# Cross attention and a decoded FFN on one core: another order for decoding, beginning and end

## What is computed

```
n = layernorm(x)
q = rmsnorm(n, ln_weight) @ w_q.T        # per head
k = ctx @ w_k.T;  v = ctx @ w_v.T
score = softmax(where(mask, q k^T + position_bias[h], -inf))
hid = x + n + (score @ v) @ w_out.T
W = NF4_CODE[w_codes] * absmax           # 512 x 512, blocks of 64
y = layernorm(hid)
out = hid + y @ W.T + 2 * (y @ W_a) @ W_b
```

## Time and profile before

| | us |
|---|---|
| median of 3 executions (860.21 to 862.35) | 860.31 |
| the profiled execution | 860.71 |
| its span in the trace | 858.9 |
| PE busy, matmuls | 832.1 (97%) |
| PE weight loads, beside them | 723.7 (84%) |
| DVE busy | 449.2 (52%) |
| ACT busy | 442.1 (51%) |
| POOL busy | 537.7 (63%) |
| PE: four LoRA matmul tiles from 3.58 and four from 7.16 | 3.78 and 3.62 |
| DVE idle ahead of the value splits at 18.42 | 4.52 |
| DVE idle ahead of `q_lo` at 786.09 (head 29), and of `row_scale`'s reciprocal at 792.40 (head 30) | 1.69 and 1.11 |
| ACT idle ahead of `qT` at 784.94 (head 29) | 3.17 |
| granted clock of PE, 42 to 46 and 77 to 81 us | 0.62 and 0.57 |

### The profile page before, as it was taken

One profiled execution on the slowest core, in us unless ns is written; L12 is line 12 of the kernel. 1 busy time (PEld: TensorE's weight loads), 2 busy tenths in 40 slices (PEclk: granted clock), 3 DMA queues, 4 the chain that ended last, 5 costly groups with the idle time before them and its releaser, 6 DMA issues.

```text
span 858.9 us, 15761 instructions
## 1 busy us (share of the span) xinstructions
PE 832.1 (97%) x4694; PEld 723.7 (84%) x4694; DVE 449.2 (52%) x761; ACT 442.1 (51%) x1296; POOL 537.7 (63%) x557
## 2 busy tenths in 40 slices
PE   8798999999999999999999999999999999999898
PEld 5687888988889888898889888898888888898776
DVE  4854656246543566246561565336562465534783
ACT  5655554354634656264543657356553646346632
POOL 0484758856686658857587557856588565865230
PEclk9999999999999999999999999999999999999999
DMA  8212323023321223113231132112220232211102
GB/s 329 73 41 89 96 70 98 19 72 102 91 65 52 89 64 95 31 61 95 68 96 56 53 106 89 37 52 92 69 95 23 69 95 75 92 40 50 44 13 86
DMA packets 51125, 64.98 MB, mean 76 GB/s; under 512 B 11008, under 2 KB 37248, under 8 KB 50080
## 3 DMA queue, kind: packets, MB, share of 16 engines
q1 hardware_dynamic: 51104, 64.73, 24.1%
HBM read 44.24 MB, written 4.19 MB: 56 GB/s over the span
## 4 chain that ended last, share of the span: by engine, by line
PE 49%; POOL 24%; ACT 11%; issue 5%; DVE 5%; SPq 3%; DMA 2%; POOLq 1%; ACTq 0%; DVEq 0%
PE w_ps L1157 23%; PE o_ps L1157 19%; POOL picked L528 8%; POOL level L531 6%; ACT p_blocks L649 4%; PE s_ps L1193 4%; POOL ring_lo L464 3%; PE s_ps L1199 3%; ACT p_blocks L600 2%; POOL wv_raw L454 2%; SPq L336 2%; POOL p L492 2%; DMA wv_raw<-wv_dram 1%; ACT kT L600 1%; POOL wo_lo L464 1%
## 5 line engine op out<-in xcount | busy, mean ns | idle before, releaser
L492 POOL TENSOR_TENSOR p<-pos_raw,mask_add 128x1024 f32<-128x1024 f32 x32 | 69.6, 2175 | 137.8 <-ACT p_blocks L649 137.3
L649 ACT ACTIVATE p_blocks<-p,neg_max 128x128 f32<-128x128 f32 x248 | 96.1, 389 | 84.0 <-DVE neg_max L966 78.6
L528 POOL TENSOR_SCALAR picked<-codes 128x256 f32<-128x256 int32 x112 | 124.4, 1111 | 19.4 <-POOL level L531 15.9
L531 POOL TENSOR_TENSOR level<-level,picked 128x256 f32<-128x256 f32 x112 | 89.6, 800 | 20.6 <-POOL picked L528 20.6
L464 POOL TENSOR_TENSOR ring_lo<-k_raw,ring_hi 128x256 fp32r<-128x256 f32 x105 | 77.0, 745 | 28.1 <-ACT ring_hi L600 25.1
L988 DVE TENSOR_TENSOR resid<-o_ps,resid 128x512 f32<-128x512 f32 x102 | 68.6, 686 | 43.2 <-PE o_ps L1157 43.2
L1157 PE MATMUL w_ps<-ctx_hi,ring_hi 128*128 128x512 f32 x210 | 84.7, 403 | 0.1
L1157 PE MATMUL w_ps<-ctx_hi,ring_lo 128*128 128x512 f32 x210 | 82.0, 391 | 0.0
L1157 PE MATMUL w_ps<-ctx_lo,ring_hi 128*128 128x512 f32 x210 | 81.7, 389 | 0.0
L600 ACT ACTIVATE p_blocks<-p_blocks,row_scale 128x128 f32<-128x128 f32 x248 | 77.1, 391 | 0.0
L600 ACT ACTIVATE ring_hi<-k_raw 128x256 fp32r<-128x256 f32 x105 | 38.8, 413 | 74.4 <-POOL k_raw L454 74.4
(11 more groups left out here) (222 smaller groups left out, 2310.8 us busy)
## 6 DMA issues: line engine op xcount, KB each, us to landing
pT<-p_blocks SPq DMA_DIRECT2D x496, 32.0 KB, 1.8
k_raw<-k_dram SPq DMA_DIRECT2D x16, 512.0 KB, 3.4
wv_raw<-wv_dram SPq DMA_DIRECT2D x8, 1024.0 KB, 4.8
q_raw<-q_dram SPq DMA_DIRECT2D x32, 256.0 KB, 3.2
wo_raw<-wo_dram SPq DMA_DIRECT2D x32, 256.0 KB, 4.0
resid<-x_dram SPq DMA_DIRECT2D x2, 1024.0 KB, 12.9
pos_raw<-pos_dram SPq DMA_DIRECT2D x32, 64.0 KB, 3.9
out_dram<-resid SPq DMA_DIRECT2D x8, 256.0 KB, 2.0
```

The costliest lines, as they stand in the source:

```text
L492: pool.tensor_tensor(p[:, :, :], pos, mask_add[:, :, :], ALU.add).then_inc(bias_done, 1)
L528: then(pool.tensor_scalar((level if code == 0 else picked)[:, :], codes[:, :], float(code), NF4[code], match, ALU.mult))
L531: then(pool.tensor_tensor(level[:, :], level[:, :], picked[:, :], ALU.add))
L649: e = act.activation(out(b), p[:, b, :].rearrange("p (k c) -> p k c", c=Q), ACT.Exp, bias=neg_max[:, b:b + 1], accum_out=prob_sum[:, b:b + 1])
```

## The change

Decoding: `PARTS` becomes 4, 4, 4 and 3 codes instead of 4, 6, 4 and 1, so two pick-and-add pairs move from j = 4 to the parts done at j = 1 and 2 (part 3 has three pairs where it had one, part 2 has other codes but as many).

```
-PARTS = ((0, 1, 2, 3), (4, 5, 6, 8, 9, 10), (11, 12, 13, 14), (15,))
-PART_STEP = (0, 7, 19, 27)
+PARTS = ((0, 1, 2, 3), (4, 5, 6, 8), (9, 10, 11, 12), (13, 14, 15))
+PART_STEP = (0, 7, 15, 23)
```

Beginning, the core of the diff by engine. PE (`EARLY_LORA` is 3, and with `parts=2` a key product waits for its second context split, `ctx_lo_done` 2 or 4, between its halves):

```
-            for c in range(C):
+            for c in range(EARLY_LORA):
                 lora_tile(c)
             pe.wait_ge(k_lo_done, PRODUCTS)
-            pe.wait_ge(ctx_lo_done, 2)
-            first_keys(1, 0)
+            pe.wait_ge(ctx_lo_done, 1)
+            first_keys(1, 0, parts=2)
             first_keys(0, 0)
...
+            for c in range(EARLY_LORA, C):
+                lora_tile(c)
             pe.wait_ge(wv_lo_done, PRODUCTS)
...
             turn_x(0)
-            first_values(3)
+            for b in (3, 4):
+                first_values(b)
             turn_x(1)
-            first_values(4)
+            first_values(5)
...
             scores(0, 1)
-            for b in range(5, B):
+            for b in (6, 7):
                 first_values(b)
```

```
             dve.wait_ge(x_loaded[0], 16)
             for b in range(HB):
                 tile_stats(b, 2 * b)
-            ask_layer_power(0)
+            ask_both(0)
+            for half_at in range(2):
+                split_first_values(half_at)
+            stage_factors(0)
...
+            residual_factors()
+            xn_low(0)
+
+            dve.wait_ge(x_turned, C)
+            context_sum(2, ctx_sum[0], ctx_raw[BLOCK_A])
             dve.wait_ge(ctx_sums, 3)
+            context_sum(4, ctx_raw[BLOCK_B], ctx_sum[1])
+            split_first(4, ctx_lo[:, 1, :, :], ctx_sum[0], ctx_hi[:, 1, :, :])
+            split_first(5, ctx_lo[:, 3, :, :], ctx_sum[2], ctx_hi[:, 3, :, :])
+            xn_low(1)
+            for b in range(HB):
+                residual(b)
+            split_first(6, ctx_lo[:, 2, :, :], ctx_sum[1], ctx_hi[:, 2, :, :])
+            for b in range(HB, B):
+                residual(b)
+            split_first(7, ctx_lo[:, 4, :, :], ctx_sum[3], ctx_hi[:, 4, :, :])
             split_q(1)
```

End. PE, and what fills the banks:

```
+        last_s = [s_ps[0][:, :, :], w_ps[2][:, :].rearrange("p (b k) -> p b k", b=HB)]
-            pe.wait_ge(attn_lo_done, 2 * (H - 2) + 2)
-            scores(H - 1, 0)
+            pe.wait_ge(attn_lo_done, 2 * (H - 2) + 1)
+            pe.wait_ge(keys_added, ADDS * PAIRS)
+            scores(H - 1, 0, last_s)
             pe.wait_ge(wo_lo_done, H - 2)
             for b in range(B):
+                if b % HB == 0:
+                    pe.wait_ge(attn_lo_done, 2 * (H - 2) + 1 + b // HB)
...
                 if b == 3:
-                    pe.wait_ge(keys_added, ADDS * PAIRS)
+                    pe.wait_ge(biased, 2 * (H - 1) + 2)
...
             for hf in range(2):
                 attend(G - 2, hf, w_ps[hf][:, :], moved)
-            for hf in range(2):
                 pe.wait_ge(last_pT_done, hf + 1)
                 attend(G - 1, hf, s_flat(hf), lambda b: last_pT[:, b, :])
```

211 lines of the change are left out of this document (103 added, 108 removed).

## The result

The changed kernel takes 841.15 us (median of four, 840.0 to 841.95) against 860.26 (also of four): a ratio of 0.9772, with an interval of 0.9751 to 0.9792, so 19.1 us or 2.3% faster. The forecast was 837.9 us, 22.4 us off.

What follows compares the result with a forecast made beforehand. PE, busy 832.1 of 858.9 us, bounds the kernel, so only its idle time and lower-clock stretches can return. 12.8 + 6.3 + 3.3 = 22.4 us off 860.7 gives 838.3, forecast as 837.9 for the median; range 834.8 to 845.0.

Steps and rivals of the forecast that it cites:

- Loop, 12.8 us: Seven group boundaries: spreading the codes removes both PE waits for value products, 1.83 us a group, bounds 11.0 and 12.9.
- All three margins: Loop: low parts ready before PE wants them, value slice 1 by 3.5 us, slice 2 near 2.7, key slice 1 2.5.
- First scores at 49.3: Beginning: PE starts head 0's scores at 49.3 instead of 54.09, 4.8 us earlier.
- sum of waits, clock, tile and product: Beginning, PE: 42.6 us less 4.95 waits and 1.4 lower clock, plus 0.9 LoRA tile and 2.72 value product: 39.9.
- factors of the first half: Beginning: staging factors of the first input half ready near 21 instead of 28.1, through earlier statistics and one power.
- What of it reaches the end, 6.3 us: Beginning: gain left after head 0's moves and head 1's exponentials, 6.3 us, bounds 4.0 and 7.8.
- lower bound of 4.0: Beginning gives only 4.0 us if DVE is stretched by 3 us or PE pays the lower clock once more.
- 0.8 us charged for DVE beside POOL: Beginning: allowance for DVE's queue ahead of head 0's scores being stretched while POOL decodes, 0.8 us.
- prediction's own sign of falling: Prediction falls if DVE takes head 0's scores over 3 us after their start, or a group's period stays above 98.
- start given back: Rival: DVE stretched beside POOL or late key roundings hold heads 0 and 1; beginning gives 2, 842.2 us; chance 0.10.
- three new waits of PE: Beginning: PE waits about 1.6 and 2.2 us in head 1's scores and 1.3 for the moves, within 71.2.
- End, 3.3: Last heads and FFN: 1.0 last scores, 1.3 softmax, 0.7 attentions by halves, 0.3 transposes; bounds 2.2 and 4.6.

Runs made afterwards that it cites:

- the second trace: The changed kernel itself, unaltered, measured and traced once more beside the others on one chip: 841.08 us, ratio 0.9778 to the kernel before.
- the first trace: One traced execution of the changed kernel at its first measurement against the kernel before: 841.15 us, ratio 0.9772.

## Why the prediction was right or wrong

- **Loop, 12.8 us: right.** 12.70 measured, alone and with the rest. All three margins came within 0.3 us of what was read from the trace of before.
- **First scores at 49.3: right** (49.03), as the sum of waits, clock, tile and product; how good each term is was not taken apart, and other executions with the new beginning have 47.9 to 50.0. The factors of the first half are ready at 20.0 instead of 21, PE's first product starts at 9.0 instead of 9.4.
- **What of it reaches the end, 6.3 us: wrong, 3.06** (3.97 in the second trace), under the lower bound of 4.0. The step that failed is the 0.8 us charged for DVE beside POOL. It was taken from two context splits, 1.74 and 1.21 us, as if a neighbour only slowed DVE down by a third. In its place stand about 1.9 us on the residual from the decoding, 1.4 us on a split from the bias tile in some executions, and 1.84 us on the row scale from the second tile. Of the last, 1.2 us reach the moves. It wasn't in the sum at all: an instruction of 0.17 us had no price that could be stretched. The moves start at 63.4 or 62.2 instead of 59.8. In the first trace these 3.6 us are 0.3 less for the scores' own start, 2.6 more until DVE takes them (5.4 us after their start, where 2.0 and the 0.8 make 2.8), and 1.2 for the row scale. The prediction's own sign of falling, more than 3 us there, came true for the beginning (5.4 and 4.7).
- The price could have been read beforehand. The prediction says that no row shows a residual instruction beside POOL, but the trace of the kernel before has one (tile `resid`): the median of the eight instructions is 0.54 us, and the first, beside POOL's key split of 71.81 to 73.00, takes 0.96.

```profile
L1064 DVE TENSOR_SCALAR resid<-resid,ln_scale,ln_shift x8: 534/536/960, 72.3 to 75.9; 128x512 f32<-128x512 f32 x8
```

- The rival "start given back" had this mechanism and gave 842.2; the time is 841.15, nearer to it than to the forecast. It got 0.10, too little: the row of 1.74 us, and the 4 us less that the prediction worked out for a residual stretched by as much, should have weighed more.
- **The three new waits of PE** (1.6, 2.2 and 1.3 us forecast) came as 4.76 and 0.93 and cost nothing, as said.
- **End, 3.3: right**, 3.04, in four pieces each within 0.4. The first was too high by 0.4, since ACT's two drains and not only the first half of the attention decide.
- The stated range of 834.8 to 845.0 holds the time.

## What to carry to other kernels

Move work to another place only after asking what the other engine on a shared resource does there: a large instruction beside a chain of small ones can hold a small one for nearly its own length, whatever the small one takes (2.00 us for 0.16 here, beside one of 2.15), and how much of that reaches the end depends on the slack behind it (1.2 us here). Fill idle time behind the step that starts a long transfer, not ahead of it: the eight residual instructions cost nothing in the gap behind the moves' start, though they took half as long again; ahead of it DVE took the first scores 4.7 and 5.4 us after their start instead of 2.0. A margin between "ready" and "wanted", read from the trace for each step that shares an engine with the moved one, forecast the gain, and roughly where it turns; what a missed margin costs has to be followed through the other engines as well.

## What was not expected of the hardware

- A VectorE instruction with two SBUF inputs doesn't end before a GpSimd addition that was ahead of it: 2.00 us for 128x4 elements (0.16 alone), 3.16 for 128x1024 (1.21 alone). It goes the other way too: GpSimd's pick takes 1.07 us, and 1.93 when it starts at 42.47 beside that split. VectorE's `scalar_tensor_tensor` with one PSUM and one SBUF input took 2.05 us for three beside the tile and without it.
- VectorE's `tensor_scalar` of 128x512, one SBUF input, took 0.53 to 0.54 us each alone, so that four started and ended within 1.90 us. Beside the decoding single ones took up to 1.00 us and four 2.58 to 3.13, and beside POOL's key splits and sums eight took 6.33.
- The beginning scatters by about 1 us from one execution to the next in the same kernel (scores of head 3 at 109.80 and 110.71), and this can change which instructions meet. POOL's decoding starts when `absmax` has landed, at 30.81 and 31.77 in these two; what else moves the start is not shown.
